# A layer norm's roots moved ahead of a multiplication in the VectorE queue of a two-layer transformer kernel

## The chip, the cores and the metric

The kernel runs on one core of a Trainium2 chip. The metric is the device time of one execution in microseconds (us), lower is better. The engines of the core are TensorE (PE), VectorE (DVE), ScalarE (ACT), GpSimd (POOL) and SyncE (SP, which issues transfers). Each works through its own list of instructions in order, and they wait for one another by semaphores.

## The reference

The input x has 8 batches of 256 tokens of 128 values. Two layers follow one another; each adds an attention and a mixture of experts, both behind a layer norm:

```python
x = x + _L0_attn_ref(_layernorm(x, axis=-1), ...)   # latent projections, rotary, 16 heads, causal softmax
x = x + _L0_ffn_ref(_layernorm(x, axis=-1), ...)    # 8 experts, two per token, gelu, layer norm behind
x = x + _L1_attn_ref(_layernorm(x, axis=-1), ...)   # chunked linear attention with retrieved states
x = x + _L1_ffn_ref(_layernorm(x, axis=-1), ...)    # 8 experts, two per token, relu

def _layernorm(x, axis=-1, eps=1e-05):
    m = jnp.mean(x, axis=axis, keepdims=True)
    v = jnp.var(x, axis=axis, keepdims=True)
    return (x - m) / jnp.sqrt(v + eps)
```

The change concerns only the first of these layer norms, the 1 / sqrt(v + eps) of its tokens.

## The kernel before

The 2048 tokens are 16 tiles of 128 (one token per partition); batch b has the tiles 2b and 2b + 1. The kernel has four stages: attention of layer 0, its experts, attention of layer 1, its experts. In the first, every engine has a loop of its own over the same written-out list of steps, `STEPS0`: pairs (c, s) of a batch counter c from -2 to 10 and a step s from 0 to 3. The loops say at which step each engine does which work of which batch, and so fix the order in each queue. Work of several batches is in flight: while the scores of batch c are made, batch c + 1 is spread and batch c + 2 normed and projected. The steps with c = -2 and -1 are the prelude, in which no scores are made yet.

One batch goes through these hands before its scores:

- DVE: moments of each tile (`moments0`: L818, L821), then the roots (`rstd0`, which calls `inv_sqrt`, L803 to L809). The root is made from integer and float operations: add eps (L803), shift right (L804), subtract from a constant (L805), and three rounds of L807, L808, L809. That makes twelve instructions, each waiting for the one ahead of it. They work on one value per token: [128 x number of tiles].
- DVE: `norm` (L832), (x - mean) * root, one instruction a tile.
- PE: `turn_x0` (L1897, a transpose), ACT: copy from PSUM (L1451), PE: `project0` (L1905, L1906, L1910), the queries and keys, each beside its rotary partner.
- DVE: `turn` (L840), two multiplications of 128x512 by the rotary table out of PSUM; this is the turning. POOL: `sum_turned` (L648) adds both halves; DVE: `round_turned` (L847) rounds the sum to `hi`; POOL: `rest_of` (L654) makes the remainder `lo`.
- PE: `spread0` (L1883 to L1889) spreads hi and lo over the heads into three PSUM banks; ACT: `key_copy` (L1463) and `stack0` (L1469) fetch them.
- PE: `max_scores` (L1835) and `masks0` (L1820, L1822); DVE: `maxima` (L859), three in each step; `split_max` (L867, L869) and `add_max` (L876). Then PE makes the scores once more (L1845, L1847), ACT the exponentials (L1483), POOL the masking (L639), PE the weighted values (L1871, L1874).

PSUM has a ring of seven banks, taken in a written-out order; whoever takes a bank waits until the bank's last content was read.

The input comes in two transfers: tiles 0 to 3 (`x_loaded[0]`), and tiles 4 to 15 (`x_loaded[1]`). The moments and roots of tiles 0 to 3 and the norms of batches 0 and 1 come ahead of the loop. In the loop, DVE does at (-2, 3) the turning of batch 0 and three casts (L912 to L914), at (-1, 0) the rounding of batch 0, the wait for `x_loaded[1]` and the moments of tiles 4 to 15, at (-1, 3) the turning of batch 1 and the roots of tiles 4 to 15, at (0, 0) the rounding of batch 1, the first maxima and the norm of batch 2, which is the first reader of these roots. POOL adds the output bias to x (L660) once a batch was normed, and at (2, 2) casts three constants (L666 to L668) behind a wait for the expert loads.

In the later stages the experts work on tiles of 128 gathered tokens: L1989 (eight matmuls, into the hidden layer) and L1997 (eight, out of it).

Of the kernel before, what the change touches and what calls it, by code (L numbers as in the profile page):

```python
# [148 lines left out]
def build(nc, inp, out, last_stage=3):  # L149
    ctx = ExitStack()  # L150
    with ctx:
# [225 lines left out]
        def inside(b):  # L377
            return 0 <= b < B
# [7 lines left out]
        def due(l, u, work):  # L386

            for u0, q in FROM[l].items():
                if u - u0 == AFTER[q >= COUNTED][work]:
                    return q  # L390
            return -1
# [87 lines left out]
        def bank0(kind, b, k=0):  # L479
            return ps[:, AT0[kind, b, k] % NRING, :]  # L480
# [308 lines left out]
        def _(dve):  # L789
# [34 lines left out]
            def rstd0(t0, t1):  # L824

                some = slice(t0, t1)
                at_start.n = inv_sqrt(rstd[:, some], mv[:, some, 1], nt1[:, 0, some], nt2[:, 0, some], LN_EPS, stats_done, at_start.n)
# [7 lines left out]
            def turn(b):  # L835

                wait(dve, "summed", b, 0)
                for n in range(2):
                    wait(dve, "proj", b, n + 1)
                    signal(dve.tensor_tensor(rot[n][:], bank0("proj", b, n), rope[:, n, :], ALU.mult), "turned")  # L840

            def round_turned(b):

                wait(dve, "sel", b, 0)
                wait(dve, "rest", b, 0)
                wait(dve, "summed", b, 1)
                signal(dve.tensor_copy(hi[:], rot[2][:]), "rounded")  # L847
# [23 lines left out]
            def add_max(b):  # L871

                for n in range(2):
                    wait(dve, "mTr", b, n + 1)
                    two = qst0[b % 3][:, 2 * n:2 * n + 2, :].rearrange("p j s -> p (j s)")
                    signal(dve.tensor_tensor(two, two.bitcast(F32), bank0("mTr", b, n), ALU.add), "max_added")  # L876
# [11 lines left out]
            def residual0(b):  # L888

                wait(dve, "outp", b, 1)  # L890
                wait(dve, "biased", b, 1)
                two = X[:, 2 * b:2 * b + 2, :].rearrange("p a d -> p (a d)")
                signal(dve.tensor_tensor(two, two, bank0("outp", b)[:, 0:2 * D], ALU.add), "residual")
                wait(dve, "residual", b, 1)
                for t in range(2):
                    signal(dve.bn_stats(stats[:, 2 * b + t, :], X[:, 2 * b + t, :]), "residual")
# [13 lines left out]
            def cast_constants():  # L910

                dve.tensor_copy(identb[:], misc[:, 0:P]).then_inc(consts_cast, 1)  # L912
                dve.tensor_copy(aboveb[:], misc[:, P:2 * P]).then_inc(consts_cast, 1)
                dve.tensor_copy(identr[:], misc[:, 0:P]).then_inc(consts_cast, 1)  # L914
# [21 lines left out]
            def take_logits(l, q, banks):  # L936

                m = ms[l]
                t0, t1 = TILES[q]
                w = D + E if l == 0 else E  # L940
                before = sum(gate_banks(l, a) for a in range(q))
                for n in range(gate_banks(l, q)):
                    dve.wait_ge(m["gated"], before + n + 1 + 1)
                    some = slice(t0 + 2 * n, t0 + 2 * n + 2) if l == 0 else slice(t0, t1)
                    h = some.stop - some.start
                    src = banks[n][:, 0:h * w].rearrange("p (t w) -> p t w", w=w)
                    if l == 0:
                        dve.tensor_copy(LG[:, some, :], src[:, :, D:D + E]).then_inc(m["logits"], 1)
                    else:
                        dve.tensor_tensor(LG[:, some, :], src, gate_b.unsqueeze(1).broadcast_to((P, h, E)), ALU.add).then_inc(m["logits"], 1)  # L950
                dve.wait_ge(m["logits"], before + gate_banks(l, q) + 1)

            def ring_banks(l, q):
                return [(bank0 if l == 0 else bank1)("gate", q, n) for n in range(gate_banks(l, q))]

            def choose(l, q, n):

                c = chains[l]
                t0, t1 = TILES[q]
                h = t1 - t0  # L960
                some = slice(t0, t1)
                wide = lambda a: a.unsqueeze(2).broadcast_to((P, h, E))
                L = LG if n == 0 else LG2
                c(dve.tensor_reduce(top[:, n, some], L[:, some, :], AX.X, ALU.max))
                c(dve.tensor_tensor(rt[0][:, some, :], L[:, some, :], wide(top[:, n, some]), ALU.is_ge))
                c(dve.tensor_tensor(rt[1][:, some, :], rt[0][:, some, :], rev_e.unsqueeze(1).broadcast_to((P, h, E)), ALU.mult))
                c(dve.tensor_reduce(top[:, 2, some], rt[1][:, some, :], AX.X, ALU.max))
                c(dve.tensor_tensor(first[:, n, some, :], rt[1][:, some, :], wide(top[:, 2, some]), ALU.is_equal))
                if n == 0:
                    c(dve.scalar_tensor_tensor(LG2[:, some, :], first[:, 0, some, :], LOWEST, LG[:, some, :], ALU.mult, ALU.add))  # L970
                else:
                    dve.tensor_tensor(picked[:, some, :], first[:, 0, some, :], first[:, 1, some, :], ALU.add).then_inc(ms[l]["picked"], 1)

            def give_slots(l, q, bank):

                m, c = ms[l], chains[l]
                t0, t1 = TILES[q]
                h = t1 - t0
                some = slice(t0, t1)
                dve.wait_ge(m["ranked"], q + 1 + 1)  # L980
                dve.tensor_tensor(ranks[:, :, some, :], first[:, :, some, :],
                                  bank[:, 0:h * E].rearrange("p (t e) -> p t e", e=E).unsqueeze(1).broadcast_to((P, TOPK, h, E)),
                                  ALU.mult).then_inc(m["slotted"], 1)
                dve.wait_ge(m["slotted"], 2 * q + 1 + 1)
                for k in range(TOPK):
                    c.add(dve.tensor_reduce(slot[:, k, some], ranks[:, k, some, :], AX.X, ALU.add))
                c.wait()
                dve.tensor_copy(sloti[:, :, some], slot[:, :, some]).then_inc(m["slotted"], 1)  # L988
# [69 lines left out]
            for c, s in STEPS0:  # L1058
                u = 4 * c + s
                q = due(0, u, "logits")  # L1060
                if q >= 0:
                    take_logits(0, q, ring_banks(0, q))
                if q >= COUNTED:
                    choose(0, q, 0)
                    choose(0, q, 1)
                q = due(0, u, "slots")
                if q >= 0:
                    give_slots(0, q, bank0("rank", q))
                if s == 3 and inside(c + 2):
                    turn(c + 2)  # L1070
                if (c, s) == (-2, 3):
                    cast_constants()
                if s == 1 and inside(c - 3):
                    residual0(c - 3)
                if (c, s) == (0, 0):
                    round_turned(1)
                if inside(c):
                    maxima(c, s)
                if s == 0 and inside(c - 1):
                    add_max(c - 1)  # L1080
                if s == 0 and inside(c + 1) and c != 0:
                    round_turned(c + 1)
                if s == 0 and FIRST // 2 <= c + 2 < B:
                    norm(c + 2)
                if (c, s) == (-1, 0):
                    dve.wait_ge(x_loaded[1], 16)
                    moments0(FIRST, NT)
                if (c, s) == (-1, 3):
                    rstd0(FIRST, NT)
                if 0 <= due(0, u, "logits") < COUNTED:  # L1090
                    choose(0, due(0, u, "logits"), 0)
                if 0 <= due(0, u, "second") < COUNTED:
                    choose(0, due(0, u, "second"), 1)
                if group(0, u) >= 0:
                    norm_rows(0, group(0, u))
                if s == 2 and inside(c - 2):
                    normalise(c - 2)
                if s == 3 and inside(c):
                    split_max(c)
                if u == PLACED[0]:  # L1100
                    place_early(0, bank0("count", COUNTED))
                if u == PLACED[0] + 1:
                    stage_first(0)
                    used_early(0)
# [1128 lines left out]
```

## Time and profile before

| | |
|---|---|
| three timed runs | 632.24, 633.45, 642.83 us |
| median | 633.45 us |
| the profiled execution | 631.0 us |
| its span, first to last instruction | 629.3 us |
| attention of layer 0 | to about 200 us |
| experts of layer 0 | about 208 to 295 us |
| attention of layer 1 | about 295 to 525 us |
| experts of layer 1 | about 528 to 629 us |

All times within the trace are counted from the start of the span. A trace is of one execution, so a duration from it is set against 631.0 us. The start of an instruction is the moment at which it had everything it waited for.

### The profile page before, as it was taken

To read this page: it belongs to the slowest core of one execution; us is meant where nothing else is said; L and a number is where in the kernel's file an instruction comes from. 1 tells how busy PE (TensorE), PEld (TensorE's weight loads), DVE (VectorE), ACT (ScalarE), POOL (GpSimd) and SP (SyncE) were. 2 spreads that over 40 slices of the span, in tenths; PEclk is the share of its full clock that TensorE was granted. 3 is DMA by queue.
4 is the path that set the end of the run, shared out by engine and by line. 5 is a ranking of instruction groups with operands and counts; after the bars stand their busy time and mean duration, and the time that the engine had idled before them with its cause. 6 is when DMAs were issued, how large, how long until landed. Compare 5 with 4: busy or idle time off the path is not lost.

```text
span 629.3 us, 14217 instructions
## 1 busy us (share of the span) xinstructions
PE 503.1 (80%) x4416; PEld 403.8 (64%) x4416; DVE 410.9 (65%) x1351; ACT 290.8 (46%) x824; POOL 267.7 (43%) x358
## 2 busy tenths in 40 slices
PE   4689998997995699994157989889889672999990
PEld 3565665654563689994056767667676462989990
DVE  5878789886657663632878666957955776453333
ACT  2234555452442466664335366625624310656650
POOL 3325443456276665454000233412732654365550
PEclk9788999995857699998565799979777755999995
DMA  7997000000001222211998000000000002223216
GB/s 231 322 312 311 2 3 1 1 10 27 1 28 39 68 68 83 75 56 64 382 306 328 2 3 1 2 1 2 28 10 2 27 28 56 62 70 86 69 39 209
DMA packets 28376, 53.72 MB, mean 85 GB/s; under 512 B 4816, under 2 KB 24208, under 8 KB 27248
## 3 DMA queue, kind: packets, MB, share of 16 engines
q1 hardware_dynamic: 23216, 42.17, 20.9%
q0 software_dynamic: 4544, 9.45, 4.2%
q10 hardware_dynamic: 544, 1.20, 0.6%
q8 instruction: 38, 0.62, 0.4%
q14 instruction: 34, 0.28, 0.2%
HBM read 42.32 MB, written 29.81 MB: 115 GB/s over the span
## 4 chain that ended last, share of the span: by engine, by line
PE 57%; DVE 28%; issue 5%; DMA 4%; ACT 2%; POOL 2%; SPq 1%; DVEq 0%; ACTq 0%; POOLq 0%
PE ps L1989 12%; PE ps L1997 11%; DVE negm L859 5%; PE ps L2089 3%; PE ps L1845 2%; DVE X L1362 2%; PE ps L2049 2%; PE ps L1871 2%; PE ps L1835 2%; DMA w<-ybuf 2%; PE ps L1980 1%; PE ps L2073 1%; PE ps L1905 1%; PE ps L1770 1%; DVE rsc L933 1%
## 5 line engine op out<-in xcount | busy, mean ns | idle before, releaser
L1569 ACT ACTIVATE probs<-ps,w1s 128x128 f32<-128x128 f32 x312 | 89.0, 369 | 48.7 <-PE ps L1989 48.5
L750 POOL DMA_INDIRECT ybuf<-yt,xg x78 | 76.4, 980 | 70.6 <-DVE yt L1116 62.8
L1989 PE MATMUL ps<-xgT,w1s 128*128 128x128 f32 x624 | 87.3, 285 | 2.3 <-ACT xgT L1560 2.2
L1997 PE MATMUL ps<-w,probs 128*128 x624 | 82.3, 276 | 0.0
L1989 PEld LDWEIGHTS ps<-xgT,w1s 128*128 128x128 f32 x624 | 80.0, 201 | 3.4 <-ACT xgT L1560 2.8
L769 POOL TENSOR_SCALAR_AFFINE_SELECT probs<-probs 128x512 f32<-128x512 f32 x64 | 39.2, 637 | 93.3 <-ACT probs L1670 93.2
L1997 PEld LDWEIGHTS ps<-w,probs 128*128 128x128 f32 x624 | 75.7, 192 | 0.1
L694 POOL DMA_INDIRECT xbuf<-rsc,sloti x64 | 62.3, 974 | 30.7 <-DVE sloti L988 15.2
L859 DVE TENSOR_REDUCE negm<-ps 128x2 f32<-128x512 f32 (+1 forms) x96 | 60.3, 685 | 22.4 <-PE ps L1822 18.2
L1483 ACT ACTIVATE probs<-ps 128x512 f32<-128x512 f32 x96 | 51.2, 603 | 38.0 <-PE ps L1845 37.7
L639 POOL TENSOR_SCALAR_AFFINE_SELECT probs<-probs 128x512 f32<-128x512 f32 x64 | 39.2, 636 | 65.5 <-ACT probs L1483 65.5
L1051 DVE COPY w1s<-w 128x516 f32 x78 | 34.5, 442 | 41.8 <-issue 36.9
L1116 DVE TENSOR_TENSOR yt<-ps,bias 128x128 f32<-128x128 f32 x78 | 22.7, 292 | 48.0 <-PE ps L1997 46.1
L1670 ACT ACTIVATE probs<-ps 128x512 f32<-128x512 f32 x64 | 34.7, 594 | 22.5 <-PE ps L2049 22.5
L1362 DVE SCALAR_TENSOR_TENSOR X<-ps,GT,X 128x128 f32<-128x128 f32 x80 | 28.0, 350 | 11.5 <-PE ps L2089 9.5
L1560 ACT ACTIVATE xgT<-ps 128x128 f32<-128x128 f32 x78 | 22.7, 292 | 20.7 <-PE ps L1980 20.7
L2049 PEld LDWEIGHTS ps<-qst,kst 32*128 32x128 f32 x256 | 19.5, 212 | 17.9 <-issue 16.3
L762 POOL TENSOR_TENSOR lo<-pqk,hi 128x512 fp32r<-128x512 f32 x6 | 7.6, 1271 | 50.7 <-DVE hi L1335 50.7
L1980 PE MATMUL ps<-misc,xg 128*128 128x128 f32 x78 | 22.8, 292 | 7.0 <-DMA xg<-xbuf 5.8
L2049 PE MATMUL ps<-qst,kst 32*128 32x128 f32 x256 | 24.1, 311 | 4.3 <-DVE pqk L1328 3.3
L2073 PE MATMUL ps<-probs,vst 128*32 128x128 f32 x512 | 24.3, 310 | 1.6 <-POOL probs L769 1.5
L1835 PE MATMUL ps<-keys,qst 32*128 32x128 f32 (+1 forms) x192 | 21.2, 330 | 4.6 <-DVE negm L859 4.4
(280 smaller groups left out, 1116.1 us busy)
## 6 DMA issues: line engine op xcount, KB each, us to landing
xbuf<-in_c_pads SPq DMA_DIRECT2D x16, 1122.0 KB, 18.9
xg<-xbuf SPq DMA_DIRECT2D x78, 66.0 KB, 1.8
w<-in_w SPq DMA_DIRECT2D x2, 2064.0 KB, 33.7
w<-in_w SPq DMA_DIRECT2D x2, 2048.0 KB, 35.7
w<-ybuf SPq DMA_DIRECT2D x8, 512.0 KB, 5.6
ybuf<-yt,xg POOLq DMA_INDIRECT x78, 2.3
probs<-in_c_sel ACTq DMA_DIRECT2D x2, 512.0 KB, 5.4
bias<-in_b SPq DMA_DIRECT2D x2, 512.0 KB, 31.1
```

What stands on the lines that cost most here:

```text
L639: last = pool.affine_select(out=diag, in_=diag, compare_op=ALU.is_ge, fill=0.0, base=0, pattern=[[0, 4], [1, P]], channel_multiplier=-1)
L694: pool.indirect_dma_start(out=xbuf[l][:, :], out_offset=bass.IndirectOffsetOnAxis(ap=sloti[:, k, t:t + 1], axis=0), in_=rsc[:, t % SLOTS, ...
L750: pool.indirect_dma_start(out=ybuf[l][:, :], out_offset=bass.IndirectOffsetOnAxis(ap=xg[n % AHEAD][:, D:D + 1].bitcast(I32), axis=0), in_= ...
L769: signal(pool.affine_select(out=chunk, in_=chunk, compare_op=ALU.is_ge, fill=0.0, base=0, pattern=[[0, 4], [1, P]], channel_multiplier=-1) ...
L859: signal(dve.tensor_reduce(dst, src, AX.X, ALU.max, negate=True), "maxed")
L1362: signal(dve.scalar_tensor_tensor(tile, bank1("look", b, look)[:, n * D:(n + 1) * D], GT[:, 2 * b + t, NC - 1 - at - n:NC - at - n], tile, ...
L1483: signal(act.activation(probs[p % 2][:, 512 * n:512 * (n + 1)], bank0("prob", p // 4, 3 * (p % 4) + n), ACT.Exp, scale=QK_SCALE), "probs_d ...
L1569: ins = act.activation(hidT[n % 3][:, c * P:(c + 1) * P], ps[:, q, c * P:(c + 1) * P], ACT.Gelu if l == 0 else ACT.Relu, bias=w[:, FF + c: ...
L1670: signal(act.activation(probs[u % 2][:, n * 4 * P:(n + 1) * 4 * P], bank1("prob", u // 4, 2 * (u % 4) + n), ACT.Copy), "probs_done")
L1989: mm = pe.matmul(ps[:, n % 2, c * P:(c + 1) * P], w[:, c * P:(c + 1) * P], xgT[n % 2][:], start=True, stop=True)
L1997: mm = pe.matmul(ps[:, 6 + n % 2, 0:D], hidT[n % 3][:, c * P:(c + 1) * P], w2[:, ds(e * FF + c * D, D)], start=(c == 0), stop=(c == FC - 1))
L2049: mm = pe.matmul(banks[n][:, j * P:(j + 1) * P], kst[b % 2][own, j, some], qst[b % 2][own, j, some], start=True, stop=True)
```

## The change

The line that bound the roots of tiles 4 to 15 to the step (-1, 3) is gone, so they belong to the block of step (-1, 0) and stand directly behind the moments in DVE's queue:

```diff
                 if (c, s) == (-1, 0):
                     dve.wait_ge(x_loaded[1], 16)
                     moments0(FIRST, NT)
-                if (c, s) == (-1, 3):
                     rstd0(FIRST, NT)
```

The order in DVE's queue was: moments of tiles 4 to 15, turning of batch 1, roots, rounding of batch 1. It is now: moments, roots, turning of batch 1, rounding of batch 1. DVE has no other work at the steps (-1, 1) and (-1, 2). The instructions themselves are the same, and the lists of the other engines are unchanged.

## Rows read from the trace of the kernel before

**Rows 1.** The page's first part and its chain by engine: busy time, share, instructions.

```profile
PE 503.1 (80%) x4416; PEld 403.8 (64%) x4416; DVE 410.9 (65%) x1351; ACT 290.8 (46%) x824; POOL 267.7 (43%) x358
...
PE 57%; DVE 28%; issue 5%; DMA 4%; ACT 2%; POOL 2%; SPq 1%; DVEq 0%; ACTq 0%; POOLq 0%
```

**Rows 2.** Timeline of DVE: start, length (us), line, operation, shapes, count, [idle before].

```profile
14.70 1.29 DVE L914 CAST identr<-misc 128x128 fp32r<-128x128 f32 x1
15.93 0.43 DVE L847 CAST hi<-rot 128x512 fp32r<-128x512 f32 x1
...
18.60 0.89 DVE L821 BATCH_NORM_AGGREGATE mv<-stats 128x2 f32<-128x6 f32 x12
21.86 1.45 DVE L840 TENSOR_TENSOR rot<-ps,rope 128x512 f32<-128x512 f32 x2 [2.37 <-PE ps L1906]
23.23 0.16 DVE L803 TENSOR_SCALAR nt<-mv 128x12 f32<-128x12 f32 x1
23.42 0.17 DVE L804 TENSOR_SCALAR rstd<-nt 128x12 int32<-128x12 int32 x1
23.63 1.15 DVE L805 TENSOR_SCALAR rstd<-rstd 128x12 int32<-128x12 int32 x1
24.81 0.17 DVE L807 SCALAR_TENSOR_TENSOR nt<-rstd 128x12 f32<-128x12 f32 x1
...
26.66 0.43 DVE L847 CAST hi<-rot 128x512 fp32r<-128x512 f32 x1
27.00 1.88 DVE L859 TENSOR_REDUCE negm<-ps 128x4 f32<-128x512 f32 x3
28.79 0.60 DVE L832 TENSOR_SCALAR xn<-X,mv,rstd 128x128 f32<-128x128 f32 x2
29.30 1.89 DVE L859 TENSOR_REDUCE negm<-ps 128x4 f32<-128x512 f32 x3
32.27 1.89 DVE L859 TENSOR_REDUCE negm<-ps 128x2 f32<-128x512 f32 x3 [1.08 <-PE ps L1822]
```

**Rows 3.** Chain that ended last, 22 to 29 us: start, length, what.

```profile
22.62 0.69 DVE rot L840
23.31 0.09 DVE nt L803
...
26.66 0.44 DVE hi L847
27.09 1.49 issue
28.59 0.55 PE ps L1883
```

**Rows 4.** Timeline of POOL.

```profile
14.60 1.30 POOL L648 TENSOR_TENSOR rot<-rot 128x512 f32<-128x512 f32 x1 [8.85 <-DVE rot L840]
...
17.66 1.42 POOL L660 TENSOR_TENSOR X<-X,bout 128x256 f32<-128x256 f32 x2
23.48 1.27 POOL L648 TENSOR_TENSOR rot<-rot 128x512 f32<-128x512 f32 x1 [4.40 <-DVE rot L840]
27.23 1.26 POOL L654 TENSOR_TENSOR lo<-rot,hi 128x512 fp32r<-128x512 f32 x1 [2.48 <-DVE hi L847]
```

**Rows 5.** Timeline of PE.

```profile
25.04 0.38 PE L1822 MATMUL ps<-aboveb,identb 128*128 128x256 bf16 x2
28.59 0.55 PE L1883 MATMUL ps<-hi,selr 128*128 128x256 f32 x1 [3.17 <-issue]
...
31.42 0.60 PE L1835 MATMUL ps<-keys,qst 32*128 32x256 f32 x6
```

**Rows 6.** Line 805 over the span; DVE by shape, 300 to 330; DVE and POOL near 323.

```profile
L805 DVE TENSOR_SCALAR rstd<-rstd x16: 170/171/1145, 6.0 to 528.8; 128x4 int32<-128x4 int32 x8, 128x2 int32<-128x2 int32 x4, 128x12 int32<-128x12 int32 x2, 128x8 int32<-128x8 int32 x1
...
L805 DVE TENSOR_SCALAR rstd<-rstd 128x12 int32<-128x12 int32 x1 | 0.2, 173 | 0.0
...
323.47 0.68 DVE L803 TENSOR_SCALAR nt<-mv 128x12 f32<-128x12 f32 x1
...
322.86 1.26 POOL L762 TENSOR_TENSOR lo<-pqk,hi 128x512 fp32r<-128x512 f32 x1 [28.47 <-DVE hi L1335]
```

**Rows 7.** Busy time by stretch (DMA share and GB/s last), then POOL's timeline.

```profile
50.00:60.00 10.00, 8.78 (x85) 5.07 (x84) 8.81 (x15) 5.18 (x11) 4.96 (x6) 0.95 0.88 366
61.00:90.00 29.00, 27.96 (x267) 18.95 (x260) 21.38 (x39) 15.40 (x34) 12.46 (x21) 0.98 0.01 2
...
65.95 1.22 POOL L639 TENSOR_SCALAR_AFFINE_SELECT probs<-probs 128x512 f32<-128x512 f32 x2 [3.75 <-ACT probs L1483]
67.12 0.29 POOL L666 CAST beforeb<-route 128x128 bf16<-128x128 f32 x1
```

**Rows 8.** Stretches again: PE, PEld, DVE, ACT, POOL busy, granted clock (1.00 is 2.4 GHz).

```profile
21.50:25.40 3.90, 3.90 (x35) 2.67 (x34) 3.29 (x8) 0.22 (x1) 1.27 (x1) 1.00 1.08 322
25.50:28.50 3.00, 0.00 (x0) 0.00 (x0) 2.79 (x10) 0.00 (x0) 1.26 (x1) 0.96 0.89 299
28.50:31.30 2.80, 2.71 (x12) 2.53 (x12) 2.69 (x6) 1.27 (x3) 0.73 (x1) 0.50 1.11 359
36.00:41.00 5.00, 2.45 (x20) 1.57 (x19) 4.90 (x11) 0.00 (x0) 0.79 (x1) 1.00 1.01 341
42.00:45.00 3.00, 3.00 (x13) 2.42 (x12) 2.37 (x4) 1.88 (x4) 2.41 (x4) 0.50 0.86 280
46.00:57.00 11.00, 10.40 (x107) 6.83 (x102) 8.67 (x14) 5.44 (x12) 4.91 (x7) 1.00 1.02 413
58.60:61.80 3.20, 3.20 (x24) 1.25 (x22) 3.12 (x4) 1.55 (x3) 2.66 (x4) 0.55 0.23 82
```

**Rows 9.** Chain that ended last, at the first tiles of the experts of layer 0.

```profile
210.72 1.71 PE ps L1989 x8
...
217.43 0.89 PE ps L1989 x8
```

## Prediction, made before the result was known

> **What bounds the kernel now.** I read the page's first two parts, then the chain that ended last, then the timelines of the stretch that the edit touches. [rows 1] show no engine that is full from end to end: PE is busy for 80% of the 629.3 us span and DVE for 65%. The chain puts 57% of the span on PE and 28% on DVE: each waits for the other in turn, so an operation on DVE costs time exactly where the chain runs through it. The edit moves twelve small DVE operations (the roots of tiles 4 to 15, L803 to L809) within the first 27 us, so the question is whether the chain runs through them, and through what it runs once they are gone.
>
> It does now. [rows 2] are the DVE queue: the moments end at 18.60 + 0.89 = 19.49, DVE then idles 2.37 us until the projections of batch 1 come from PE, multiplies them at 21.86 and 22.62 (L840, the turning), does the roots from 23.23 to 26.62, and only then rounds batch 1 (L847) at 26.66. [rows 3] are the chain there: PE's projection, the second turning, the roots, the rounding, and after it, as "issue", the 1.49 us in which POOL makes the rest (L654). [rows 4] show POOL: its sum of the two turned halves (L648), for which L847 waits, runs from 23.48 to 24.75. [rows 5] show PE: no matmul between 25.42 and 28.59, where the spread (L1883) starts 0.10 after POOL's L654 ends (27.23 + 1.26 = 28.49).
>
> **The change, part by part.** Nothing is added or taken away: twelve DVE instructions over twelve columns, no DMA, no new wait on another engine. They go past one thing in the DVE queue, the turning of batch 1.
>
> *The removal behind the turning.* The chain holds the roots from 23.31 to 26.66, 3.35 us [rows 3]. But L847 can't move up by that much, for it waits for POOL's L648, which ends at 24.75 [rows 4]. With 0.05 from POOL's end to DVE's start (the first pair shows 0.03: L648 ends at 15.90, L847 stands at 15.93 [rows 2, 4]) it starts at 24.80. So of the 3.35 us, 24.80 - 23.31 = 1.49 were hidden behind POOL, and 26.66 - 24.80 = **1.86 us** is what the path gives back. If the cover weren't there, the gain would be the full 3.35.
>
> *The addition ahead of the turning.* Behind the moments the roots would start at about 19.51. Their pitch: 23.42 - 23.23 = 0.19 and 23.63 - 23.42 = 0.21 for the first two, from 24.81 to 26.66 for the last nine, 1.85. The third, L805, took 1.15 at 23.63, but of its 16 executions the median is 0.171 and the other one of twelve columns took 0.173 [rows 6]. What does the long one have beside it? POOL's L648, 23.48 to 24.75: L805 ends at 24.78. The same pair is seen at L803 at 323.47, whose end at 324.15 is that of POOL's L762 (322.86 + 1.26 = 324.12), and at L914, 14.70 to 15.99, beside POOL's 14.60 to 15.90 [rows 2, 4, 6]. Between 19.08 and 23.48 POOL does nothing [rows 4], so I take L805 at 0.17, with 0.03 to the next. Sum: 0.19 + 0.21 + 0.20 + 1.85 = 2.45, so the roots end at 21.96. The first turning starts at 21.98 instead of 21.86; the second waits for PE until 22.62 anyway, and 21.98 + 0.69 = 22.67. The roots thus lie in the 2.37 us idle and stick out by 0.12, at most 0.05 of which reaches the second turning and POOL. I take 0 for it in the sum and leave 0.05 for the range. Without that idle time they would cost 2.45 on the path, since both turnings stand behind them.
>
> The Trainium skill, Advanced Engine Details and Errata, section VectorE Performance Modes, says that the second Vector SBUF port is shared with GpSimd, so that two-port Vector instructions and GpSimd instructions block one another. By that rule L805 was long for POOL's sake, the roots take 2.45 in a place where POOL is idle, and the sum is the forecast's; were the 1.15 the instruction's own, it would be that of rival 3, 1 us more. The trace speaks for the rule with 1.145 against 0.173 us.
>
> *What follows L847.* Is something else late then? Its rest on POOL moves to 25.36 and ends at 26.63, the spread on PE starts at 26.73 instead of 28.59. PE has finished what it can do before, at 25.42 [rows 5], and the three maxima (L859) behind L847 read banks that PE filled by then, so they too start 1.86 earlier (27.00 to 25.14). norm (L832) of batch 2, which reads the roots first, goes from 28.79 to 26.93, long behind them. The second and third bank of the spread need the first two maxima read: 25.14 + 1.3 = 26.4, in time. What stands behind, the maxima at 32.27, turning, split, max correction, is a DVE and PE chain without a DMA in it [rows 2, 5], so it slides by 1.86 as one piece.
>
> *Fixed points.* Only a transfer could eat the gain. The loads keep the DMA engines 88% busy from 50 to 60 us and 1% behind 61 [rows 7]; the first work that needs the expert weights' loads is POOL's cast at 67.12, which follows its predecessor without a wait (65.95 + 1.22 = 67.17) [rows 7]. It would go to 65.3, still five microseconds behind the loads. I cost this at 0; were it not so, the gain would be lost as a whole.
>
> *TensorE's clock.* The granted clock is the one thing that could change sizes behind the edit. It is at 2.4 GHz from 21.5 to 28, at 1.2 GHz from 28.5 to 31.3 after PE's 3.17 us of no work, again at 1.2 from 42 to 45 after the thin stretch from 36 to 41 [rows 5, 8]. Afterwards PE's pause before the spread is 26.73 - 25.42 = 1.31 instead of 3.17. Two bounds. If the spread then runs at 2.4 GHz, PE is ready before the banks are: at present it comes to the scores at 31.42, while the maxima that free their last bank end at 29.30 + 1.89 = 31.19 [rows 2, 5], so that at most 0.23 more is gained, 2.09 in all. If the slow stretch stays where it is in time while the work moves up, the scores and the first mask between 31.42 and 32.27, 0.85 us at 2.4 GHz, fall into it and take 0.85 longer; less the 0.23, the gain falls to 1.2. Nearest to the row of now, the slow stretch goes along with the spread: 1.86, with 1.2 and 2.09 as ends.
>
> The Trainium skill, TensorE: Matmul & The Clock Gate, section The HAM clock gate, says that the moment of the change isn't tied to the kernel's start, which makes it vary from run to run. One trace can't show that; if it holds, each of the two ends happens in some executions.
>
> **Sum.** The profiled execution took 631.0 us (span 629.3, 1.7 around it). It would take 631.0 - 1.9 = 629.1. The three timed runs have a median of 633.45, which is 2.45 above it; the middle of all four (631.0, 632.24, 633.45, 642.83) is 632.85. From that middle: 632.85 - 1.86 = **631.0 us**, 0.3% less than before.
>
> **Rivals.**
> 1. *The spread stays at 2.4 GHz and later slow stretches go too.* At once 2.09 are gained; where the chain is PE's, a slow batch of eight matmuls of an expert (L1989) costs 1.71 against 0.89 [rows 9], 0.82 each. One fewer: 2.91 in all, 629.9. For it: PE's pause shrinks from 3.17 to 1.31. Against it: a slow stretch came also at 58.6 to 61.8, with PE 10.40 of 11 us busy before it [rows 8].
> 2. *Slower: the clock's pattern shifts against the expert tiles.* [rows 9] show the first two tiles of the experts at 1.71 us for eight matmuls. Whoever starts them earlier relative to the clock's rise has more of them slow. It decides at three more slow groups, 3 x 0.82 = 2.46 against 1.86: +0.6, 633.5. Against it: the pause of PE before the experts, from which the slow clock comes, is the same length and moves with the rest.
> 3. *The root is slow by itself on twelve columns* and takes 1.15 there too: roots until 22.94, turning at 22.96 and about 23.6, ending at 24.3; POOL ends at 25.7; L847 at 25.8; gain 0.85, 632.0. Against it are the 0.173 and the three pairs.
> 4. *Nothing reaches the end*: a wait that I don't see is bound to the clock on the wall, 632.85. Against it are the fixed points above.
>
> **Chances.** Forecast 0.60, rival 1 0.14, rival 2 0.12, rival 3 0.06, rival 4 0.08. The forecast's own range is a gain of 2.09 from the lowest execution, 631.0, to one of 1.2 from the timed median, 633.45: 628.9 to 632.25. All cases lie within 1% of the time before, so the range is governed by how executions differ: the lowest known less rival 1 gives 631.0 - 2.91 = 628.1, taken as 628.0; the timed median plus rival 2, with half a microsecond for a middle that falls elsewhere, 633.45 + 0.6 + 0.5 = 634.5. About 2 in 10 stays out, mainly for a middle run like the one of 642.83. A measurement of this kernel can tell about 2%, 12.7 us, from no change; the largest gain of any case is 3 us and even the full 3.35 isn't a quarter of that. Faster by over 2%: 0.01; within 2%: 0.97; slower by over 2%: 0.02, for a clock pattern that settles badly in many places.
>
> **What would show it.** In the profile of the changed kernel: L805 of twelve columns at 0.17; the roots over by 22.0; turnings at about 21.98 and 22.65; POOL's L648 starting by 23.5; L847 within 0.1 of its end, at 24.8; the spread at 26.7; the maxima that now stand at 32.27 between 30.1 and 30.9; the roots gone from the chain, and POOL's L648 in their place. The prediction is wrong on the size if L847 stands later than 25.2, and on the carry if the first expert matmuls, now at 210.72, stand less than 1 us earlier.

## The result and the profile after

| | before | changed |
|---|---|---|
| median of 22 executions each, side by side | 636.16 us | 628.01 us |
| lowest, highest | 631.15, 647.73 | 623.99, 643.26 |
| profiled execution (span) | 631.0 (629.3) | 627.99 (626.3) |

The ratio of the changed kernel to the one before is 0.9882, with a 95% interval of 0.9854 to 0.9911: 5.7 to 9.3 us faster at 636.16 us. That is below the 2% that count as a clear change here, but clear of zero, and four times the forecast 1.86 us. (The ratio leaves out executions more than 1.5% above the fastest of their kernel, so the means over all executions that are given below can differ from it.) Lines behind L1086 have moved up by one in the changed kernel, so L1883 of before is L1882, and so on.

DVE around the edit, from the timeline of the changed kernel (start, length, line, operation; against [rows 2]):

```profile
18.59 0.89 DVE L821 BATCH_NORM_AGGREGATE mv<-stats 128x2 f32<-128x6 f32 x12
19.51 0.18 DVE L803 TENSOR_SCALAR nt<-mv 128x12 f32<-128x12 f32 x1
19.72 0.17 DVE L804 TENSOR_SCALAR rstd<-nt 128x12 int32<-128x12 int32 x1
19.93 0.17 DVE L805 TENSOR_SCALAR rstd<-rstd 128x12 int32<-128x12 int32 x1
...
21.78 0.17 DVE L809 SCALAR_TENSOR_TENSOR rstd<-nt,rstd 128x12 f32<-128x12 f32 x1
22.11 1.46 DVE L840 TENSOR_TENSOR rot<-ps,rope 128x512 f32<-128x512 f32 x2 [0.16 <-PE ps L1905]
25.14 0.43 DVE L847 CAST hi<-rot 128x512 fp32r<-128x512 f32 x1 [1.57 <-POOL rot L648]
25.48 1.88 DVE L859 TENSOR_REDUCE negm<-ps 128x4 f32<-128x512 f32 x3
```

The roots lie in the idle time and end at 21.95. L805 takes 0.17 us, not 1.15. DVE even waits 0.16 for PE before the turning. The rounding waits for POOL alone. The chain (start, length, what) has POOL's sum where the roots stood in [rows 3]:

```profile
22.88 0.70 DVE rot L840
...
23.74 1.28 POOL rot L648
25.02 0.03 issue
25.05 0.05 DVEq L362
25.10 0.04 issue
25.14 0.43 DVE hi L847
```

PE's timeline at the spread, against [rows 5]: the pause is 1.40 us instead of 3.17, and a matmul stands every 0.12 us instead of every 0.21:

```profile
25.30 0.38 PE L1821 MATMUL ps<-aboveb,identb 128*128 128x256 bf16 x2
27.08 0.36 PE L1882 MATMUL ps<-hi,selr 128*128 128x256 f32 x1 [1.40 <-issue]
27.27 0.28 PE L1883 MATMUL ps<-lo,selr 128*128 128x256 f32 x1
27.39 0.28 PE L1887 MATMUL ps<-hi,selr 128*128 128x256 f32 x1
27.50 0.28 PE L1888 MATMUL ps<-lo,selr 128*128 128x256 f32 x1
```

The spread of batch 5, far down the same stage, stands 1.90 us earlier. First before, then the changed kernel:

```profile
96.73 0.39 PE L1883 MATMUL ps<-hi,selr 128*128 128x256 f32 x1
```

```profile
94.83 0.39 PE L1882 MATMUL ps<-hi,selr 128*128 128x256 f32 x1
```

So at 95 us this pair of traces has the 1.9 us of the forecast, though not by its account: the rounding and the spread of batch 1 came only 1.5 us earlier (25.14 against 26.66, 27.08 against 28.59), and 0.4 us were added on the way. At 211 us the changed kernel is half a microsecond *behind* before (first expert matmuls at 211.26 against 210.72), and at the end 3.0 us ahead. The granted clock goes with both. The clock of both in the same stretches (PE, PEld, DVE, ACT, POOL busy; granted clock, where 1.00 is 2.4 GHz and 0.50 is 1.2; DMA), first before, then changed:

```profile
25.00:62.00 37.00, 30.07 (x236) 20.57 (x235) 31.28 (x59) 12.49 (x26) 14.33 (x18) 0.87 0.91 322
62.00:100.00 38.00, 36.47 (x345) 24.46 (x344) 30.42 (x61) 20.83 (x46) 17.03 (x26) 1.00 0.01 2
100.00:205.00 105.00, 87.83 (x752) 56.71 (x750) 77.84 (x231) 43.72 (x92) 54.48 (x81) 0.82 0.05 16
205.00:530.00 325.00, 254.00 (x2320) 212.68 (x2320) 216.93 (x818) 155.54 (x454) 127.73 (x167) 0.81 0.23 75
```

```profile
25.00:62.00 37.00, 31.52 (x255) 21.74 (x254) 29.91 (x51) 14.10 (x30) 14.56 (x19) 0.91 0.93 322
62.00:100.00 38.00, 36.49 (x356) 23.80 (x349) 32.01 (x69) 20.73 (x45) 17.15 (x26) 1.00 0.01 2
100.00:205.00 105.00, 88.31 (x729) 56.90 (x727) 76.89 (x221) 42.35 (x89) 53.80 (x81) 0.79 0.05 16
205.00:530.00 325.00, 247.66 (x2326) 208.52 (x2327) 218.42 (x825) 156.08 (x456) 130.86 (x172) 0.83 0.24 77
```

In the first stretch the changed kernel has the better clock, in the third the worse one, in the fourth the better one again. Between the first transposes of the two expert stages (L1980 of before) it took 318.0 us against 321.6, which is where it goes from behind to ahead. One trace of each can't explain a difference of the medians of 8 us. The experiments look for what the average over executions rests on.

### The profile page after: what moved, and what is told of

It reads as the page before. It is cut to its first block, busy times and chain, and to the rows that moved or that the text cites. A ratio compares the mean times of both kernels' runs of the same rounds, so it can differ in the third digit from the quotient of the medians.

```text
span 626.3 us, 14216 instructions
## 1 busy us (share of the span) xinstructions
PE 497.1 (79%) x4416; PEld 399.1 (64%) x4416; DVE 411.0 (66%) x1351; ACT 291.1 (46%) x824; POOL 268.4 (43%) x358
## 4 chain that ended last, share of the span: by engine, by line
PE 55%; DVE 29%; issue 5%; DMA 4%; ACT 2%; POOL 2%; SPq 1%; DVEq 0%; ACTq 0%; POOLq 0%
PE ps L1988 12%; PE ps L1996 11%; DVE negm L859 5%; PE ps L2088 3%; DVE X L1361 2%; PE ps L1844 2%; DMA w<-ybuf 2%; PE ps L1834 2%; PE ps L1870 2%; PE ps L1979 1%; PE ps L1904 1%; DVE rsc L933 1%; PE ps L2048 1%; PE ps L2072 1%; PE ps L1905 1%
## 5 line engine op out<-in xcount | busy, mean ns | idle before, releaser
L1482 ACT ACTIVATE probs<-ps 128x512 f32<-128x512 f32 x96 | 51.4, 601 | 38.9 <-PE ps L1844 38.5
L639 POOL TENSOR_SCALAR_AFFINE_SELECT probs<-probs 128x512 f32<-128x512 f32 x64 | 39.2, 636 | 67.9 <-ACT probs L1482 67.8
L2048 PEld LDWEIGHTS ps<-qst,kst 32*128 32x128 f32 x256 | 17.7, 193 | 16.6 <-issue 14.8
L1834 PE MATMUL ps<-keys,qst 32*128 32x128 f32 (+1 forms) x192 | 23.0, 344 | 4.9 <-DVE negm L859 4.6
L2048 PE MATMUL ps<-qst,kst 32*128 32x128 f32 x256 | 22.0, 291 | 4.7 <-DVE pqk L1327 3.7
```

What stands on the lines that cost most here:

```text
L639: last = pool.affine_select(out=diag, in_=diag, compare_op=ALU.is_ge, fill=0.0, base=0, pattern=[[0, 4], [1, P]], channel_multiplier=-1)
L1482: signal(act.activation(probs[p % 2][:, 512 * n:512 * (n + 1)], bank0("prob", p // 4, 3 * (p % 4) + n), ACT.Exp, scale=QK_SCALE), "probs_d ...
L1834: pe.matmul(bank[:, part * w:(part + 1) * w], qst0[b % 3][own, js[part], t * P:(t + 1) * P], keys0[b % 3][own, 0:w], start=(part == 0), st ...
L2048: mm = pe.matmul(banks[n][:, j * P:(j + 1) * P], kst[b % 2][own, j, some], qst[b % 2][own, j, some], start=True, stop=True)
```

## The experiments

Three theories. **A**: the slide is the forecast's, and PE's long pause at 25 to 28 us brings on slow stretches of the clock, which lengthen the prelude; a shorter pause spares them. **B**: there is the slide and nothing else. **C**: the gain isn't from the rounding's earlier place but from something else in the changed program. Later **D** came in: each edit shifts all work by a fraction of a microsecond, and with that where the clock's slow stretches fall in the later stages.

**Only the attention of layer 0.** Both kernels were ended behind it (`build(nc, aps, out, last_stage=0)`, with one more line changed so that the semaphores of the experts are still counted up at the start).

> The kernel before, ended behind the attention of layer 0 (the two expert stages and the attention of layer 1 are left out, so its output is not the reference's). It is the base for the run att0_after. Both theories: about 200 us, since the attention of layer 0 ends near 200 in the trace of before. No statement on the difference from this run alone.

> The changed kernel, ended at the same place as att0_before. Theory A (a piece of 1.5 to 1.9 us slides up, and TensorE's clock pays the rest within the same stage, because the long pause of PE at 25 to 28 us is what starts the first slow stretches): 4 to 8 us less than att0_before. Theory B (the piece slides by 1.9 us, and all above that arises in later stages): 1.5 to 2.5 us less. Theory C (the slide is lost again at the clock's next slow stretch, and the 7 us of the whole kernel come from elsewhere): less than 1 us of difference.

Measured: 220.8 us (219.54 to 226.53, 7 executions) and 220.79 us (213.63 to 224.3, 6 executions). The medians are equal, the means 222.7 and 220.1, each uncertain by more than 1 us. Inconclusive: this stage alone varies by 7 to 11 us between executions of the same kernel. The expected 200 us left out what follows the attention: the last scatter of rows starts at 217.91 in att0_before. The traces are of use, though. In the one of att0_before, batch 5's spread stood at 101.4, 4.7 us later than in the whole kernel's trace, with the same instructions up to there; in that of att0_after it stood at 94.7.

**The roots twice, at the new place and at the old.**

```diff
                 if (c, s) == (0, 0):
+                    rstd0(FIRST, NT)
                     round_turned(1)
```

(on the changed kernel)

> The changed kernel with the roots of tiles 4 to 15 done a second time at their old place, behind the turning of batch 1 and ahead of its rounding. The work at the new place stays, the rounding stands as late as before (26.7 us). Theories A and B: the whole gain comes from the rounding's earlier place, so this run is as slow as the kernel before, ratio 0.997 to 1.003. Theory C: the gain has its cause elsewhere, such as in the changed program, and stays: ratio 0.988 to 0.992.

> The kernel of the run twice once more (roots at the new and at the old place). Its first ratio, 0.994 [0.990, 0.998], lay between both answers. Theories A and B (the rounding's place carries all): ratio 0.997 to 1.003, and over 4 us more than after_again on the same chip. Theory C (the cause is elsewhere in the changed program): within 2 us of after_again.

Measured: ratio 0.994 [0.9896, 0.9984] and, on another chip, 0.9949 [0.9906, 0.9992]. In the trace of twice all is as in before around the edit, 0.2 us later: L805 takes 1.15 again beside POOL's L648, and the rounding stands at 26.86 (in twice_again at 27.51, since PE's projection came later in that execution).

```profile
23.83 1.15 DVE L805 TENSOR_SCALAR rstd<-rstd 128x12 int32<-128x12 int32 x1
...
26.86 0.43 DVE L847 CAST hi<-rot 128x512 fp32r<-128x512 f32 x1
```

The ratios lie between the answers, but they decide little: both intervals reach into the range of A and B (0.997 to 1.003) and into that of C (0.988 to 0.992). Over all 12 executions each, the means are 631.0 against 634.8 us of before (3.9 less, uncertain by 1.6) and 632.4 against 632.6 (0.2 less, uncertain by 1.8). So the local gain is gone, and whether a part of the gain in the whole stays is not shown. After both results theory D took shape.

**The changed kernel again**, beside twice_again on one chip.

> The changed kernel once more, beside twice_again, so that the two are compared on one chip. All theories: ratio to the kernel before 0.985 to 0.992, as measured.

Measured: 627.33 us, ratio 0.9904 [0.9863, 0.9946]; twice_again 630.73. The gain is there a second time, on another chip; twice_again lies 3.4 us above it, with an uncertainty of about 2 us on the difference of the means, which neither shows nor excludes the over 4 us of A and B, or C's 2. Over all executions the mean of after_again is 628.9 us, 3.6 below before's 632.6 and uncertain by 1.6; the ratio's 0.9904 would be 6.1 us. The size of the gain on this chip thus lies between the two.

**The roots behind the rounding**, so that PE's spread starts early but DVE's maxima late.

```diff
                 if (c, s) == (0, 0):
                     round_turned(1)
+                    rstd0(FIRST, NT)
...
                     moments0(FIRST, NT)
-                    rstd0(FIRST, NT)
```

(against the changed kernel; lines left out at the dots)

> The roots of tiles 4 to 15 behind the rounding of batch 1 and ahead of its first maxima. The spread on PE starts as early as in the changed kernel (26.7 us), but the maxima on DVE start later than in the kernel before, since one of the twelve operations meets POOL's L654: 25.2 + 3.4 = 28.6 against 27.0. Theory A (PE's pause and with it the clock is what pays): faster than before, ratio 0.990 to 0.995. Theory B (the chain of maxima on DVE sets the time): 1.6 us slower than before, ratio about 1.0025.

Measured: 639.16 us, ratio 1.0068 [1.0026, 1.0109], 4.3 us slower. DVE has the roots from 25.46 to 28.82, again with a 1.11 us L805, here beside POOL's L654. PE starts the spread at 27.05, and then stands for want of a bank that the late maxima must free:

```profile
27.05 0.36 PE L1882 MATMUL ps<-hi,selr 128*128 128x256 f32 x1 [1.40 <-issue]
27.25 0.28 PE L1883 MATMUL ps<-lo,selr 128*128 128x256 f32 x1
29.60 0.58 PE L1887 MATMUL ps<-hi,selr 128*128 128x256 f32 x1 [2.08 <-DVE negm L859]
```

A's expected gain failed, since the pause was only moved, not spared. B's direction was right; its size (1.6 us) lies at the edge of the interval, which is 1.7 to 6.9 us. The maxima start 1.9 us later (28.86 against 27.00), and batch 5's spread stands 7.2 us behind that of before (103.94 against 96.73). The clock in between is the lowest of all runs:

```profile
25.00:62.00 37.00, 30.36 (x181) 20.47 (x180) 26.37 (x52) 10.19 (x22) 10.11 (x12) 0.72 0.89 314
```

So in this pair a delay of 1.9 us has grown by 5.3 us within 75 us. That pair exaggerates, since before's trace is the earliest of its kind (96.7; the five traces with a late rounding have 98.7 on average, see below), against which behind_round is 5.2 us late. The growth goes with the clock, in the direction opposite to the change's.

**PE's pause filled.** Twelve matmuls of 128x512 in the pause of the kernel before, into the bank BO, which isn't read before it is overwritten:

```diff
+            def fill(n):
+
+                for _ in range(n):
+                    pe.matmul(ps[:, BO, :], identb[:], aboveb[:].unsqueeze(1).broadcast_to((P, 4, P)), start=True, stop=True)
...
+                if (c, s) == (0, 1):
+                    fill(12)
                 if s == 1 and inside(c + 1):
                     spread0(c + 1)
```

> The kernel before, with 12 matmuls of 128x512 on PE in its pause of 3.17 us ahead of the spread of batch 1; their result goes to a bank that nobody reads before it is overwritten. They take 12 x 0.215 = 2.6 us, so nothing else moves, and the roots stay at their old place. Theory A (the pause brings the slow clock on, and that makes the piece behind it 2 to 4 us longer): 3 to 6 us less than before, ratio 0.991 to 0.995, and the first slow stretch at 28 us is gone or shorter. Theory B (the slide of 1.9 us is the local gain and the clock does nothing on average): ratio 1.000, within 0.003.

Measured: 635.89 us, ratio 1.0025 [0.9989, 1.006]. No gain; A in its simple form is refuted. In its trace the slow stretch at 28 to 31 us is gone, as expected, but behind PE's next pauses (0.86 and 1.68 us, from 37.3 and 39.6) came another from 40.3 to 47.1, and a long one from 57.4 to 67.6. The clock over 25 to 62 us was 0.84, no better than the 0.87 of before. Filling one pause of three took away one slow stretch and not the others.

**All three pauses filled**, with the roots at the new place (5, 3 and 6 matmuls) and at the old (12, 3 and 6); the second group stands ahead of `turn_max(0)`, the third ahead of the first `prob_scores0`.

> The changed kernel with such matmuls in its three pauses of PE between 25 and 39 us: 5 in the one of 1.40 us, 3 in the one of 0.87, 6 in the one of 1.69. Theory A: 2 to 5 us less than after_again, ratio to before 0.980 to 0.985. Theory B: as after_again, 0.988.

> The kernel of the run after_fill once more, since its first timing rests on 6 executions: changed kernel, PE's three pauses between 25 and 39 us filled with 5, 3 and 6 matmuls. Theory A (PE's pauses in the prelude bring slow stretches on, which lengthen the piece up to 60 us): ratio to before 0.980 to 0.988 again, and no slow stretch between 25 and 60 us. Theory D (where the slow stretches fall is settled by fractions of a microsecond all along the attention, so every edit draws anew): any ratio from 0.985 to 0.995.

> The kernel before with all three pauses filled (12, 3 and 6 matmuls), the roots at their old place. Against after_fill_again this is the change alone, with the clock held at its fast level in the prelude. Theory A: the spread of batch 5, at 96.7 to 101.4 us in the traces with the roots at their old place, comes at 95.5, 1.9 behind after_fill's 93.6; the time is 1.9 us above after_fill_again, ratio to before 0.985 to 0.991. Theory D: the spread of batch 5 comes at 95.5 too, but the time of the whole may be up to 5 us on either side of that, since later stretches are drawn anew: ratio 0.985 to 1.003.

Measured: after_fill 623.35 us, ratio 0.9861 [0.9811, 0.991]; after_fill_again 625.67, 0.9892 [0.9843, 0.994]; before_fill3 627.77, 0.9842 [0.9783, 0.99], the last two on one chip, 6 executions each. In none of the three traces is there a slow stretch between 25 and 100 us. Busy time and clock by stretch, in before_fill3:

```profile
25.00:62.00 37.00, 34.03 (x279) 21.78 (x276) 31.46 (x61) 14.17 (x31) 14.61 (x19) 1.00 0.92 323
62.00:100.00 38.00, 36.44 (x349) 23.73 (x348) 32.26 (x69) 20.49 (x44) 17.41 (x26) 1.00 0.01 3
```

This is the strongest result. With the roots where they were, filling the pauses alone gives about as much as the change: ratio 0.9842, and 627.3 against 634.0 us (0.989) in the mean of all executions. Since the filling leaves every other instruction as it was, the slow clock behind PE's pauses does cost this kernel time: 6.7 us in these means, uncertain by 2.0. Batch 5's spread came at 94.60, earlier than the 95.5 expected, against 93.6 and 92.47 with both. The change on top of the filling is 1.0 to 2.1 us at that point, which is the forecast's slide, and can't be told from zero in the whole: the means of before_fill3 and after_fill_again are 627.3 and 626.5, uncertain by 1.9 and 1.2.

**A small delay** ahead of the rounding, 0.2 us in the kernel before, 0.8 us in the changed one, by one or four operations whose result isn't used (the edit of before_late; after_late has `range(4)`):

```diff
                 if (c, s) == (0, 0):
+                    wait(dve, "summed", 1, 1)
+                    for _ in range(1):
+                        at_start(dve.tensor_scalar(nt1[:, 0, FIRST:NT], mv[:, FIRST:NT, 1], LN_EPS, None, ALU.add))
                     round_turned(1)
```

> The kernel before with one more small DVE operation (0.2 us, its result is not used) ahead of the rounding of batch 1, which so stands at 26.86 as in the run twice instead of 26.66. Theory A and the forecast's own account: 0.2 us more than before, ratio 1.000 within the noise. Theory D: 0.2 us are enough for another draw; as the run twice measured 0.994 and 0.995 with its rounding at that very place, the ratio here is 0.993 to 0.997 as well.

> The changed kernel with four small DVE operations (4 x 0.2 us) ahead of the rounding of batch 1, so that it stands at about 25.9, half way between the changed kernel (25.1) and before (26.7). Theory A: half of the gain, ratio 0.993 to 0.996. Theory D: not between the two but anywhere from 0.985 to 1.005.

Measured: before_late 633.08 us, 0.9973 [0.9943, 1.0003]; after_late 634.51 us, 1.0006 [0.997, 1.0042], both with 12 executions on one chip. The first can't be told from 1 nor from what D expected. Its rounding stood at 27.74 in the trace, not at the 26.86 expected, since PE's projection came later in this execution: an execution shifts this place by more than the 0.2 us of the edit. The second is telling: 0.8 us of delay, and the gain is lost as a whole, though by the slide alone half should have stayed. D's wide range held it, but would have held nearly anything.

The trace of after_late doesn't show where the gain is lost. The spread of batch 1 ran at the slow clock, a matmul every 0.21 us, as in before:

```profile
27.52 0.55 PE L1885 MATMUL ps<-hi,selr 128*128 128x256 f32 x1 [2.42 <-issue]
27.87 0.41 PE L1886 MATMUL ps<-lo,selr 128*128 128x256 f32 x1
```

But only 0.44 us of the longer pause (2.42 against 1.40) is a later spread; the other 0.58 is PE having finished earlier in this execution. POOL's sum was 0.28 us earlier too, so the rounding stood at 25.59, not at the 25.9 expected. And batch 5's spread stands at 94.95, where the changed kernel has 94.83.

## What the runs say together

For each trace: the distance from the spread of batch 1 to that of batch 5, in which all these kernels do the same work (but for the filling matmuls, and the roots in behind_round), and how many microseconds at 1.2 GHz fell into it.

| kernel | spread of batch 1 | of batch 5 | distance | slow clock in it |
|---|---|---|---|---|
| after_fill, after_fill_again, before_fill3 | 28.0, 26.8, 28.9 | 93.6, 92.5, 94.6 | 65.6, 65.7, 65.7 | 0 |
| changed kernel, att0_after | 27.1, 27.0 | 94.8, 94.7 | 67.8, 67.7 | 6.8 |
| after_again | 28.1 | 96.0 | 67.9 | 6.8 |
| after_late | 27.5 | 95.0 | 67.4 | 10.2 |
| before, twice | 28.6, 28.8 | 96.7, 96.9 | 68.1, 68.1 | 9.9, 10.0 |
| before_late | 29.7 | 98.9 | 69.2 | 13.7 |
| twice_again | 29.4 | 99.6 | 70.1 | 13.7 |
| att0_before | 29.6 | 101.4 | 71.8 | 17.1 |
| before_fill | 29.4 | 100.1 | 70.7 | 17.1 |
| behind_round | 27.1 | 103.9 | 76.9 | 23.9 |

With no slow clock the distance is 65.7, the same to 0.1 us in three runs. With slow clock it grows by 0.2 to 0.5 us for each slow microsecond (2.1 for 6.8, 6.1 for 17.1, 11.2 for 23.9, of which 2.1 are the wait for the bank). The five traces with the rounding at 26.66 to 27.74 (before, att0_before, twice, twice_again, before_late) have their batch 1 at 29.2 on average, and their batch 5 at 98.7. The three with the changed order have 27.4 and 95.2. So at batch 5 the change is worth 3.5 us on average, uncertain by 1.0: 1.8 from an earlier batch 1, and 1.7 with less slow clock in the piece. The profile of before was one of the lucky executions of its kernel in this piece, which is why its trace shows only 1.9.

The mean granted clock is on record for every execution, not only the profiled ones (but for the 22 of before in the result). The means over all executions, uncertain by 0.6 to 1.9 us and 0.001 to 0.004:

| kernel | mean time | mean granted clock |
|---|---|---|
| before, on three chips | 634.8, 632.6, 634.0 | 0.838, 0.842, 0.840 |
| changed, on two | 629.1, 628.9 | 0.849, 0.850 |
| after_fill, after_fill_again, before_fill3 | 623.9, 626.5, 627.3 | 0.861, 0.854, 0.854 |
| twice, twice_again | 631.0, 632.4 | 0.843, 0.845 |
| before_late, after_late | 632.8, 633.6 | 0.840, 0.843 |
| before_fill | 635.0 | 0.837 |
| behind_round | 639.3 | 0.832 |

The changed kernel ran at a higher clock than before; the kernels that lost its gain, or most of it, lie close to before or between the two. Within the kernels too, an execution whose clock is higher by 0.01 is shorter by about 3.7 us (an estimate, a line through all these executions with one slope). By it the 0.008 to 0.011 that separate the changed kernel from before are worth some 3 to 4 us. That is a connection and not yet a cause; the filled kernels are what shows that the clock moves the time.

## Why the prediction was right or wrong

The measured time, 628.01 us, lies just inside the stated range of 628.0 to 634.5, and the change is faster within 2%, as said; but as a difference the forecast of 0.3% was a quarter of the measured 1.2%. That the time fell inside, by 0.01 us, is luck: the base was 3.3 us too low (632.85 against a median of 636.16) and the gain 6.3 us too small (1.86 against 8.15 between the medians), and the two offset one another in part. The lower bound was that of rival 1 and not of the forecast, whose own range ended at 628.9.

- *The roots sit in idle time and escape POOL.* Right. 21.95 against the 21.96 worked out, L805 at 0.17. Two further runs put them beside a POOL operation, and L805 took 1.15 and 1.11 there: rival 3 is refuted.
- *The rounding then waits for POOL's sum, so 1.86 of 3.35 us are given back.* Right in mechanism, small miss in size: the rounding is at 25.14, 1.52 us earlier in this pair. 0.26 of the missing 0.34 is PE's second projection, for which the second turning stood at 22.88 instead of 22.62 in this execution; the rest is the way from POOL's end to DVE's start, 0.13 and not 0.05.
- *The slide is carried as one piece.* Not as it was meant. The 1.90 us at batch 5 are close to the 1.86 by chance: 1.51 from the earlier spread of batch 1, and 0.39 from a piece behind it that was shorter with 6.8 us of slow clock instead of 9.9. At the first expert matmuls the changed kernel was 0.54 us later (211.26 against 210.72), where the prediction had named less than 1 us earlier as the sign of being wrong on the carry. It was: what happens behind the edit moves by several microseconds with the clock. POOL's cast stands at 65.27 as forecast, without a wait.
- *TensorE's clock, 1.2 to 2.09 as the ends.* This is the term that was mis-sized. The text took PE's pause of 3.17 us as the cause of one slow stretch of 2.8 us and priced only the first scores behind it. It should have priced the whole prelude: without slow clock the piece to batch 5 is 65.7 us long, and in the kernel before it was 68.1 to 71.8. There were 2.4 to 6.1 us to be had there, and on average the change took 1.7 of them besides the slide. The middle case was wrong too: the slow stretch did not go along with the spread, which ran at the fast clock in the changed kernel.
- *Rival 1* (2.91 us, given 0.14) was nearest: the spread stayed at 2.4 GHz and a later slow stretch went. But it priced a single group of eight matmuls. *Rival 2* is not seen: the first two expert tiles took 1.71 us in both kernels, the third 1.40 before and 1.35 changed. *Rival 4* is refuted, since the gain is clear of zero.
- *The base.* One profile and three timed runs were too few: beside the 22 executions of the kernel before in the result (631.15 to 647.73), the profiled one would be the fastest. Chips differ besides: the medians of before on the three chips of the experiments were 635.0, 632.55 and 633.56.

What stays open: the traces account for 3.5 us up to batch 5, and the gain of the whole is 7.5 and 6.1 us by the two ratios, 8.0 and 3.6 by the means of all executions. Where the rest arises is not shown. From batch 5 to the experts' first transpose the kernels with the old order took 108.0 to 112.6 us and the changed one 115.0 and 112.5 (the filled ones 107.8 to 116.7). From there to the first transpose of the second expert stage the changed order took 317.9 to 318.5 us in four traces, filled ones included, but 322.5 in after_late; the others lie anywhere from 314.4 to 325.3. The last stage is the same in all, 98.0 to 98.7 us. One trace of each kernel can't say whether executions of the changed kernel fare better there on average. Why after_late loses the whole gain is open as well.

No version is shown to beat the changed kernel: the intervals of the filled ones (0.9842 to 0.9892) overlap its own (0.9882, 0.9904). On the one chip where both ran, though, the mean of after_fill is 5.0 us below that of after_again, uncertain by 1.9, and theory A had expected 2 to 5.

## What to carry to other kernels

Put small dependent work into an idle stretch ahead of an operation on the path rather than behind it, and subtract what another engine (here POOL's sum) would have made the successor wait anyway. In a stage where PE has pauses of 1 to 3 us, price a shorter or longer pause by the granted clock of the whole stage, at both levels, and not by the matmuls directly behind it: filling three such pauses was worth some 7 us here, and 0.8 us of delay went with the loss of the change's whole gain. And where executions of one kernel differ by 10 us, take the base from many of them, compare the granted clock of all executions, and check from one trace only what is local.

## What the runs showed of the hardware that was not expected

- An operation on [128 x 12] on DVE (L805) took 0.17 us alone and 1.15, 1.15 and 1.11 us (before, twice, behind_round) beside a POOL operation on two inputs, ending within 0.04 us of it each time. This is the sharing of the port that the Trainium skill describes in Advanced Engine Details and Errata, section VectorE Performance Modes, and the trace agrees. A float operation on two inputs is held as well: L869 on [128 x 32] took 0.22 us alone and 1.22 at 72.20 in before, beside POOL's L648 from 72.07 to 73.35. L807 to L809 never ran beside such an operation in these traces.
- The slow clock came back after PE pauses of no more than 1.7 us, when two stood close together (35.0 to 35.9 and 37.3 to 39.0 us in the changed kernel, then slow from 38.9 to 45.7). Twelve matmuls in the largest pause of the kernel before took away the stretch behind it and not the later ones; 21 in all three removed them up to 100 us.
